# Summing a chunk's weighted neighbour rows and its accumulator on VectorE instead of TensorE, in the two four-head graph attention layers

## The chip, the cores and the metric

One core of a Trainium2 chip runs the whole program. The metric is the device time in microseconds (us) of one execution, the median of several.

## What is computed

A graph has 3,125 nodes with 256 features and 53,125 edges (`src`, `dst`). The reference runs four blocks, each added to `x`: an eight-head graph attention, a mixture-of-experts network with eight experts, two four-head graph attention layers, and a small gated network. Only the two four-head layers are changed:

```python
h = (h_in @ W).reshape(n, 4, 64)
alpha_s = jnp.sum(h * a_s, axis=-1)
alpha_d = jnp.sum(h * a_d, axis=-1)
e = jax.nn.leaky_relu(alpha_s[src] + alpha_d[dst], 0.2)
m = segment_max(e, dst, num_segments=n)
ex = jnp.exp(e - m[dst])
alpha = ex / segment_sum(ex, dst, num_segments=n)[dst]
out = segment_sum(h[src] * alpha[:, :, None], dst, num_segments=n)
return out.reshape(n, 4 * 64) + b
```

So for each node and head: a softmax over the node's neighbours, and the sum of their 64 features weighted by it.

## The kernel before

Nodes are sorted by degree into 25 tiles of 128, one node to a partition. A tile's neighbours are taken in **rounds**: a round is one neighbour of each of the 128 nodes, fetched by one indirect DMA (128 rows of 268 numbers: four heads of 64 features and a one, then the two attention terms). Up to four rounds of one tile make a **chunk** (`ROUNDS` = 4, `TAIL_ROUNDS` = 3), and four chunks, one for each of the four buffer slots (`SLOTS`), make a **block**. A layer has 30 blocks: 21 with chunks of four rounds, then 9 with chunks of three, 120 chunks and 444 gathers. The function `attend` does this for all three attention layers. With `qk` true it is the eight-head layer, with `qk` false one of the four-head layers, which bear the names `gt0` and `gt1` (the profile writes `gt` for both).

The softmax is computed as the chunks come: `peak` holds each node's running maximum and `acc` its running weighted sum, 4 heads by 65 (the last of the 65 is the sum of the weights themselves). What happens to a chunk, by engine:

- GpSimd (POOL) issues its three or four gathers into `rows[:, k]` (line 934), once `weighted` says that the chunk four before, in the same slot, has been read.
- ScalarE (ACT) waits for a slot's gathers, tells VectorE through `chunk_ready`, and issues the load of the slot's next list of indices (`hand_over`, lines 1116 to 1118, 869). Later it computes the exponentials of the shifted scores (line 1132) into `exps`. At a block's end it loads the next list of tiles (line 876). It hands slot k+1 over before it does the exponentials of slot k.
- VectorE (DVE) works in the order that `block_of` writes out by hand. In the step of chunk k it begins the scores of k (lines 981, 987), weights the rows of chunk k-1 into `wv` (`weight_chunk`, line 1014), finishes k's raw scores (line 997), rescales the accumulator of chunk k-2 by the exponential of the change of its peak (`rescale`, line 1027), takes the new peak of k (line 1003), adds chunk k-2's sum to the accumulator (`accumulate`, line 1033) and shifts k's scores (lines 1008, 1009).
- TensorE (PE) sums a chunk's rounds: for each round a product of the identity with `wv[:, k, r]`, accumulated in PSUM in `part` (`sum_block`, line 1183). In float32 the profile shows two matrix instructions for each product.

The accumulator is thus touched three times in a chunk: rescaled in SBUF, summed apart in PSUM by PE, and added.

In `block_of` the rounds of the chunk weighted at k = 0 are always taken as `ROUNDS`, since that chunk belongs to the block before. After a layer, `part` also serves the projection to the next layer (lines 1198 and 1206), and `norm_group` divides by the sum of the weights.

Of the kernel before, what the change touches and what calls it, by code (L numbers as in the profile page):

```python
# [6 lines left out]
ALU, ACT, AX = mybir.AluOpType, mybir.ActivationFunctionType, mybir.AxisListType  # L7

P = 128
# [13 lines left out]
SLOTS = 4  # L23
# [784 lines left out]
def attend(nc, c, g, name, heads, own, own_rows, table, width, qk, bias_row=None, begin=None, onward=None):  # L808
# [13 lines left out]
    ROUNDS, TAIL_ROUNDS = g.rounds, g.rounds - 1  # L822
    MIN_FULL, MAX_FULL = chunk_limits(ROUNDS)
    first_wv, handing = 1 if qk else 0, not qk
    h, dh = heads, D // heads
    av = dh + 1
# [4 lines left out]
    with Mem(nc, name) as m:  # L831
# [4 lines left out]
        idx = m.sb("idx", [P, SLOTS, ROUNDS], I32)  # L836
        listed = m.sb("listed", [1, LISTS * SLOTS, 2], I32)
        score = m.sb("score", [P, SLOTS, ROUNDS + 1, h])
        wv = m.sb("wv", [P, SLOTS, ROUNDS + (1 if qk else 0), h, av])
        recip = m.sb("recip", [P, 2, NT, h])  # L840
        part = m.ps("part", [P, SLOTS, 512])
        exps = None if qk else m.ps("exps", [P, SLOTS, 64])
# [35 lines left out]
        with nc.Block(no_gpsimd_drain=True) as block:  # L878
# [72 lines left out]
            def _(dve):  # L951
# [19 lines left out]
                full, blocks = blocks_of(dve)  # L971
# [39 lines left out]
                def weight_chunk(k, n, rounds):  # L1011
                    dve.wait_ge(exped, n)
                    if not qk:
                        dve.tensor_tensor(wv[:, k, 0:rounds, :, :], rows[:, k, 0:rounds, 0:HW].rearrange("p r (h f) -> p r h f", f=av),  # L1014
                                          exps_of(k)[:, 1:rounds + 1, :].unsqueeze(3).to_broadcast([P, rounds, h, av]), ALU.mult).then_inc(weighted, 1)
                        return
                    row, w = rows[:, k, 0:dve_rounds, v0:v0 + D], wv[:, k, 1:dve_rounds + 1, :, :]
                    dve.tensor_tensor(w[:, :, :, 0:dh], row.rearrange("p r (h d) -> p r h d", d=dh),
                                      w[:, :, :, dh:dh + 1].to_broadcast([P, dve_rounds, h, dh]), ALU.mult).then_inc(weighted, 1)

                def rescale(k, n, t):


                    a = acc[:, bass.ds(t, 1), :, :].rearrange("p a h f -> p (a h) f")
                    dve.wait_ge(added, n)
                    factor = wv[:, k, 0, :, dh:dh + 1] if qk else exps_of(k)[:, 0, :].unsqueeze(2)
                    dve.tensor_tensor(a, a, factor.to_broadcast([P, h, av]), ALU.mult).then_inc(rescaled, 1)

                def accumulate(k, n, t):
                    a = acc[:, bass.ds(t, 1), :, :].rearrange("p a h f -> p (a h f)")  # L1030
                    dve.wait_ge(rescaled, n)
                    dve.wait_ge(part_sum, n)
                    dve.tensor_tensor(a, a, part[:, k, 0:h * av], ALU.add).then_inc(added, 1)  # L1033

                def block_of(i, first, rounds):


                    n = [k + 1 if first else dve.snap(i * SLOTS + (k + 1)) for k in range(SLOTS)]
                    at = 0 if first else dve.snap(i % LISTS * SLOTS)
                    dve.wait_ge(list_in, 32 if first else i * 16 + 16)  # L1040
                    t = [tile_at(at)]
                    for k in range(SLOTS):
                        one, two = (k - 1) % SLOTS, (k - 2) % SLOTS
                        begin_scores(k, n[k], t[k], rounds)
                        if not (first and k < 1):
                            weight_chunk(one, n[k] - 1, rounds if k else ROUNDS)

                        if k < SLOTS - 1:
                            t.append(tile_at(at + (k + 1)))
                        sum_scores(k, n[k], rounds)  # L1050
                        if not (first and k < 2):
                            t_two = t[k - 2] if k >= 2 else tile_at((i + (LISTS - 1)) % LISTS * SLOTS + (SLOTS + k - 2))
                            rescale(two, n[k], t_two)
                        raise_peak(k, n[k], rounds)
                        if not (first and k < 2):
                            accumulate(two, n[k], t_two)
                        shift_scores(k, n[k], t[k], rounds)

                block_of(0, True, ROUNDS)
                if qk:  # L1060
                    dve.wait_ge(own_rest, 16 * (groups - 1))
                with dve.Fori(1, full) as i:
                    block_of(i, False, ROUNDS)
                with dve.Fori(full, blocks) as i:
                    block_of(i, False, TAIL_ROUNDS)
                last = dve.snap(blocks * SLOTS)
                weight_chunk(SLOTS - 1, last, TAIL_ROUNDS)
                for back in (1, 0):
                    t_back = tile_at((blocks + (LISTS - 1)) % LISTS * SLOTS + (SLOTS - 1 - back))
                    rescale(SLOTS - 1 - back, last + (2 - back), t_back)  # L1070
                    accumulate(SLOTS - 1 - back, last + (2 - back), t_back)
                dve.wait_ge(added, last + 3)

                dve.tensor_scalar(recip[:, 0, :, :], acc[:, :, :, dh], 1.0e-30, None, ALU.max).then_inc(den, 1)
# [97 lines left out]

            @block.tensor
            def _(pe):
                pe.sem_inc(part_sum, 2)

                def sum_block(i, rounds):
                    for k in range(SLOTS):
# [5 lines left out]
                                             start=(r == 0), stop=(r == rounds - 1))  # L1184
                        last.then_inc(part_sum, 1)

                full, blocks = blocks_of(pe)
                with pe.Fori(0, full) as i:
                    sum_block(i, ROUNDS)
                with pe.Fori(full, blocks) as i:  # L1190
                    sum_block(i, TAIL_ROUNDS)

                def turn_tile(t):
                    pe.wait_ge(normed if qk else gelued, t // GROUP + 1)
# [1218 lines left out]
```

## Time and profile before

| | us |
|---|---|
| median of 3 runs | 3762.15 |
| lowest and highest of them | 3753.01, 3766.68 |
| span of the profiled execution | 4117.1 |
| gathers of gt0, first to last | 2455.2 to 3129.4 |
| gathers of gt1, first to last | 3199.6 to 3876.5 |

| engine | busy us in the span | share |
|---|---|---|
| PE | 2568.9 | 62% |
| DVE | 2297.6 | 56% |
| POOL | 1687.9 | 41% |
| ACT | 1376.2 | 33% |

The page gives no other time of the profiled execution than its span, so this is its own time. It is 355 us longer than the median of the runs without a profile. The busy times are of the whole program; the two changed layers take the stretch from about 2,450 to 3,890 us, without the projection between them.

### The profile page before, as it was taken

The numbers are of one execution on the slowest core, as the hardware profiler recorded it, in microseconds if no ns is written. First come the engines' busy times: TensorE is split into PE (matmuls) and PEld (weight loads), VectorE is DVE, ScalarE is ACT, GpSimd is POOL, SyncE is SP. The second block draws the span as 40 slices with busy tenths as digits, with TensorE's granted clock in tenths as the row PEclk, the third lists the DMA queues.
The fourth block names the chain that finished last, engine by engine and source line by source line (L and its number), as shares of the span: only waits on it lengthen the run. The fifth ranks groups of instructions, "written<-read, shape, count | busy, mean of one in ns | idle before, by whom it ended". The sixth has DMA issues, their size and how long they took to land. (4 is left out here: it accounts for less than half of the span.)

```text
span 4117.1 us, 65520 instructions
## 1 busy us (share of the span) xinstructions
PE 2568.9 (62%) x14664; PEld 1816.4 (44%) x14665; DVE 2297.6 (56%) x6774; ACT 1376.2 (33%) x4120; POOL 1687.9 (41%) x1822
## 2 busy tenths in 40 slices
PE   7668884987355455645999734444545345445499
PEld 4455233821233333435999623333334233333288
DVE  5867996798577777753111234444455444445642
ACT  1035941587576774311444310000001000000144
POOL 0102001030577676530222356666654666665411
PEclk9579975999676776756999856666677666667689
DMA  4066002811666666422222124333332333333200
GB/s 150 20 167 171 15 3 66 220 64 43 199 181 176 176 177 172 124 78 61 78 76 77 55 84 91 93 88 94 89 88 66 91 91 90 94 90 83 65 27 18
DMA packets 258271, 399.97 MB, mean 97 GB/s; under 512 B 101152, under 2 KB 182606, under 8 KB 257942
## 3 DMA queue, kind: packets, MB, share of 16 engines
q0 software_dynamic: 96144, 291.26, 25.8%
q1 hardware_dynamic: 125814, 103.95, 9.2%
q10 hardware_dynamic: 36240, 3.89, 0.7%
q8 instruction: 34, 0.56, 0.1%
q14 instruction: 39, 0.32, 0.0%
HBM read 355.41 MB, written 43.54 MB: 97 GB/s over the span
## 5 line engine op out<-in xcount | busy, mean ns | idle before, releaser
L1183 PE MATMUL gt_part<-gt_wv,all_ident 128*128 128x260 f32 x1776 | 649.6, 532 | 746.5 <-DVE gt_wv L1014 677.5
L934 POOL DMA_INDIRECT gt_rows<-h_rows,gt_idx x888 | 839.7, 946 | 524.3 <-DVE gt_wv L1014 266.9
L1183 PEld LDWEIGHTS gt_part<-gt_wv,all_ident 128*128 128x128 f32 x1776 | 452.4, 267 | 943.7 <-DVE gt_wv L1014 761.9
L934 POOL DMA_INDIRECT att_rows<-kv_rows,att_idx x444 | 468.0, 1054 | 350.3 <-issue 175.7
L1183 PE MATMUL att_part<-att_wv,all_ident 128*128 128x264 f32 x888 | 339.6, 546 | 369.1 <-ACT att_wv L1137 187.9
L1183 PEld LDWEIGHTS att_part<-att_wv,all_ident 128*128 128x128 f32 x888 | 225.8, 268 | 482.9 <-issue 337.8
L1014 DVE TENSOR_TENSOR gt_wv<-gt_rows,gt_exps 128x1040 f32<-128x1040 f32 (+1 forms) x240 | 280.4, 1168 | 221.1 <-ACT gt_exps L1132 156.0
L1137 ACT ACTIVATE att_wv<-att_rows,att_wv 128x32 f32<-128x32 f32 x1632 | 367.9, 308 | 71.8 <-issue 51.0
L1132 ACT ACTIVATE gt_exps<-gt_score 128x20 f32<-128x20 f32 (+1 forms) x240 | 45.5, 190 | 767.2 <-issue 444.7
L1132 ACT ACT_TABLE_LOAD x63 | 80.8, 1283 | 551.1 <-issue 550.8
L1489 PE MATMUL ex_up<-ex_xe,ex_w 128*128 128x128 f32 x1760 | 208.4, 278 | 12.7 <-DVE ex_xe L1453 12.7
L1489 PEld LDWEIGHTS ex_up<-ex_xe,ex_w 128*128 128x128 f32 x1760 | 207.5, 194 | 16.5 <-DVE ex_xe L1453 13.1
L1498 PE MATMUL ex_down<-ex_w,ex_hid 128*128 128x256 f32 x880 | 199.1, 380 | 0.0
L985 DVE TENSOR_TENSOR att_prod<-att_rows,at_own 128x1056 f32<-128x1056 f32 (+1 forms) x120 | 142.4, 1186 | 79.5 <-SPq L888 45.3
L731 PE MATMUL ixcs_window<-ixcs_oh_c,ixcs_oh_p 128*128 128x512 f16 x416 | 164.3, 418 | 23.8 <-ACT ixcs_oh_p L716 9.6
L716 ACT ACTIVATE ixcs_oh_p<-ixcs_oh_l,edges_value_of_d 128x128 f16<-128x128 f16 x416 | 165.8, 401 | 26.3 <-DVE ixcs_oh_c L669 11.4
L731 PE MATMUL ixcd_window<-ixcd_oh_c,ixcd_oh_p 128*128 128x512 f16 x416 | 160.7, 395 | 18.7 <-ACT ixcd_oh_p L716 3.0
L1498 PEld LDWEIGHTS ex_down<-ex_w,ex_hid 128*128 128x128 f32 x880 | 163.3, 191 | 19.5
L716 ACT ACTIVATE ixcd_oh_p<-ixcd_oh_l,edges_value_of_s 128x128 f16<-128x128 f16 x416 | 165.5, 402 | 17.9 <-DVE ixcd_oh_c L669 6.3
L1033 DVE TENSOR_TENSOR gt_acc<-gt_acc,gt_part 128x260 f32 x240 | 102.0, 425 | 121.5 <-issue 54.4
L1511 ACT ACT_TABLE_LOAD x55 | 70.6, 1283 | 275.5 <-PE ex_up L1489 275.5
L1453 DVE TENSOR_SCALAR ex_xe<-ex_turn,ex_ln_g,ex_ln_b 128x128 f32<-128x128 f32 x112 | 40.8, 406 | 200.0 <-PE ex_turn L1474 179.8
(511 smaller groups left out, 5203.5 us busy)
## 6 DMA issues: line engine op xcount, KB each, us to landing
ex_w<-in_W SPq DMA_DIRECT2D x16, 1024.0 KB, 7.4
ixbs_parts_bc<-key_parts_s SPq DMA_DIRECT2D x14, 1024.0 KB
ixbs_parts_bc<-key_parts_s SPq DMA_DIRECT2D x28, 512.0 KB, 6.2
ixbd_parts_bc<-key_parts_d SPq DMA_DIRECT2D x14, 1024.0 KB
ixbd_parts_bc<-key_parts_d SPq DMA_DIRECT2D x28, 512.0 KB
gt_rows<-h_rows,gt_idx POOLq DMA_INDIRECT x888
att_rows<-kv_rows,att_idx POOLq DMA_INDIRECT x444
y_rows<-ex_y POOLq DMA_DIRECT2D x55, 128.0 KB, 2.0
```

The lines of the kernel that those rows point to most:

```text
L716: act.activation(oh_p[k % RING][:, :], oh_l[k % RING][:, :], ACT.Copy, scale=values[:, bass.ds(i * BATCH + k, 1)]).then_inc(valued, 1)
L731: pe.matmul(window[:, :], oh_p[k % RING][:, :], oh_c[k % RING][:, :], start=False, stop=True, skip_group_check=True).then_inc(summed, 1)
L934: pool.indirect_dma_start(out=rows[:, k, r, :], out_offset=None, in_=table, in_offset=bass.IndirectOffsetOnAxis(ap=idx[:, k, r:r + 1], axi ...
L985: dve.tensor_tensor(of_row, row[:, :, 0:D + h], q, ALU.mult).then_inc(multiplied, 1)
L1014: dve.tensor_tensor(wv[:, k, 0:rounds, :, :], rows[:, k, 0:rounds, 0:HW].rearrange("p r (h f) -> p r h f", f=av), exps_of(k)[:, 1:rounds + ...
L1033: dve.tensor_tensor(a, a, part[:, k, 0:h * av], ALU.add).then_inc(added, 1)
L1132: act.activation(wv[:, k, 0:rounds + 1, :, dh] if qk else exps_of(k)[:, 0:rounds + 1, :], score[:, k, 0:rounds + 1, :], ACT.Exp).then_inc( ...
L1137: last = act.activation(wv[:, k, r + 1, e, 0:dh], rows[:, k, r, v0 + e * dh:v0 + (e + 1) * dh], ACT.Copy, scale=wv[:, k, r + 1, e, dh:dh + 1])
L1183: last = pe.matmul(part[:, k, 0:h * av], c.ident[:, :], wv[:, k, first_wv + r, :, :].rearrange("p h f -> p (h f)"), start=(r == 0), stop=( ...
L1489: last = pe.matmul(up[:, q // 2, (q % 2) * P:(q % 2 + 1) * P], w1[:, k, h, q * P:(q + 1) * P], xe[:, h, :], start=(h == 0), stop=(h == KC ...
L1498: last = pe.matmul(out, hid[:, q, :], w2[:, k, q, :], start=(q == 0), stop=(q == HC - 1))
L1511: act.activation(hid[:, q, :], up[:, q // 2, (q % 2) * P:(q % 2 + 1) * P], ACT.Gelu, bias=b1[:, bass.ds(e, 1), q]).then_inc(act_done, 1)
```

## The change

For the four-head layers (`not qk`):

- `wv` gets one more plane for each slot, behind the rounds.
- `rescale` writes the rescaled accumulator into that plane, and no longer in place.
- `accumulate` is one `tensor_reduce` over the rounds and that plane, written to the accumulator. Its innermost axis is the round, so that it reads one number of each plane in turn, 260 numbers (1,040 bytes) apart.
- PE's loops over the blocks are gone, and with them the semaphore `part_sum`.
- The functions are told how many rounds the chunk has (`before` is the number for a chunk of the block before). For that, the first block of three-round chunks is written out ahead of the loop over the others. The chunk weighted at k = 0 in those others now has three rounds.

The eight-head layer keeps its instructions.

```diff
-        wv = m.sb("wv", [P, SLOTS, ROUNDS + (1 if qk else 0), h, av])
+        wv = m.sb("wv", [P, SLOTS, ROUNDS + 1, h, av])
...
-                def rescale(k, n, t):
+                def rescale(k, n, t, rounds):
                     a = acc[:, bass.ds(t, 1), :, :].rearrange("p a h f -> p (a h) f")
                     dve.wait_ge(added, n)
-                    factor = wv[:, k, 0, :, dh:dh + 1] if qk else exps_of(k)[:, 0, :].unsqueeze(2)
-                    dve.tensor_tensor(a, a, factor.to_broadcast([P, h, av]), ALU.mult).then_inc(rescaled, 1)
+                    if not qk:
+                        dve.tensor_tensor(wv[:, k, rounds, :, :], a, exps_of(k)[:, 0, :].unsqueeze(2).to_broadcast([P, h, av]), ALU.mult).then_inc(rescaled, 1)
+                        return
...
-                def accumulate(k, n, t):
+                def accumulate(k, n, t, rounds):
                     a = acc[:, bass.ds(t, 1), :, :].rearrange("p a h f -> p (a h f)")
+                    if not qk:
+                        dve.wait_ge(state_set, 3)
                     dve.wait_ge(rescaled, n)
+                    if not qk:
+                        dve.tensor_reduce(a, wv[:, k, 0:rounds + 1, :, :].rearrange("p r h f -> p (h f) r"), AX.X, ALU.add).then_inc(added, 1)
+                        return
                     dve.wait_ge(part_sum, n)
                     dve.tensor_tensor(a, a, part[:, k, 0:h * av], ALU.add).then_inc(added, 1)
...
-                            weight_chunk(one, n[k] - 1, rounds if k else ROUNDS)
+                            weight_chunk(one, n[k] - 1, rounds if k else before)
...
-                with dve.Fori(full, blocks) as i:
-                    block_of(i, False, TAIL_ROUNDS)
+                if qk:
+                    with dve.Fori(full, blocks) as i:
+                        block_of(i, False, TAIL_ROUNDS, ROUNDS)
+                else:
+                    block_of(full, False, TAIL_ROUNDS, ROUNDS)
+                    with dve.Fori(dve.snap(full + 1), blocks) as i:
+                        block_of(i, False, TAIL_ROUNDS, TAIL_ROUNDS)
...
-                pe.sem_inc(part_sum, 2)
+                if qk:
+                    pe.sem_inc(part_sum, 2)
...
-                full, blocks = blocks_of(pe)
-                with pe.Fori(0, full) as i:
-                    sum_block(i, ROUNDS)
-                with pe.Fori(full, blocks) as i:
-                    sum_block(i, TAIL_ROUNDS)
+                if qk:
+                    full, blocks = blocks_of(pe)
+                    with pe.Fori(0, full) as i:
+                        sum_block(i, ROUNDS)
+                    with pe.Fori(full, blocks) as i:
+                        sum_block(i, TAIL_ROUNDS)
```

The lines of the changed kernel lie a few below those of before: the rescaling is line 1025, the reduction line 1035.

How VectorE's step stands in the loop over blocks of four-round chunks of layer `gt0` (`gat_own` is the layer's own table, ISA rows are waits and register work), before:

```order
L981 COPY gt_score<-gt_peak 128x4
L987 ISA
L987 TENSOR_TENSOR gt_prod<-gt_rows,gat_own 128x16
L1014 TENSOR_TENSOR gt_wv<-gt_rows,gt_exps 128x1040
L997 SCALAR_TENSOR_TENSOR gt_score<-gt_prod 128x16
L1027 ISA
L1027 TENSOR_TENSOR gt_acc<-gt_acc,gt_exps 128x260
L1003 TENSOR_REDUCE gt_new_peak<-gt_score 128x4
L1033 TENSOR_TENSOR gt_acc<-gt_acc,gt_part 128x260
L1008 TENSOR_TENSOR gt_score<-gt_score,gt_new_peak 128x20
L1009 COPY gt_peak<-gt_new_peak 128x4
```

And now:

```order
L981 COPY gt_score<-gt_peak 128x4
L987 ISA
L987 TENSOR_TENSOR gt_prod<-gt_rows,gat_own 128x16
L1014 TENSOR_TENSOR gt_wv<-gt_rows,gt_exps 128x1040
L997 SCALAR_TENSOR_TENSOR gt_score<-gt_prod 128x16
L1025 ISA
L1025 TENSOR_TENSOR gt_wv<-gt_acc,gt_exps 128x260
L1003 TENSOR_REDUCE gt_new_peak<-gt_score 128x4
L1035 TENSOR_REDUCE gt_acc<-gt_wv 128x260
L1008 TENSOR_TENSOR gt_score<-gt_score,gt_new_peak 128x20
L1009 COPY gt_peak<-gt_new_peak 128x4
```

No instruction has moved and there are as many as before: the rescaling has another target, and the addition from PSUM has become the reduction, ahead of the shift (line 1008) that ScalarE's exponentials wait for.

PE's loop over the blocks of four-round chunks of layer `gt0`, before:

```order
L1188 UNCONDITIONAL_BRANCH
L1188 ISA
L1183 MATMUL gt_part<-gt_wv,all_ident 128x260 x4
L1179 REGISTER_ALU
L1183 MATMUL gt_part<-gt_wv,all_ident 128x260 x4
L1179 REGISTER_ALU
L1183 MATMUL gt_part<-gt_wv,all_ident 128x260 x4
L1179 REGISTER_ALU
L1183 MATMUL gt_part<-gt_wv,all_ident 128x260 x4
L1188 ISA
L1188 COMPARE_AND_BRANCH
```

And now, PE's rows from the end of the work ahead of the layer (line 1545) on:

```order
L1545 UNCONDITIONAL_BRANCH
L1183 UNCONDITIONAL_BRANCH
L1210 MATMUL gt_part<-all_ident,gat_own 128x128 x4
L1218 MATMUL gt_part<-all_ga,gt_a_t 128x264 x2
L1210 MATMUL gt_part<-all_ident,gat_own 128x128 x2
```

Both loops are gone from PE, and its first work in the layer is the projection (lines 1210 and 1218 now, 1198 and 1206 before).

## Rows read from the trace of the kernel before

**Rows 1.** The page's costliest groups: instructions, busy us and mean ns, idle before.
```profile
L1183 PE MATMUL gt_part<-gt_wv,all_ident 128*128 128x260 f32 x1776 | 649.6, 532 | 746.5 <-DVE gt_wv L1014 677.5
L1014 DVE TENSOR_TENSOR gt_wv<-gt_rows,gt_exps 128x1040 f32<-128x1040 f32 (+1 forms) x240 | 280.4, 1168 | 221.1 <-ACT gt_exps L1132 156.0
L1033 DVE TENSOR_TENSOR gt_acc<-gt_acc,gt_part 128x260 f32 x240 | 102.0, 425 | 121.5 <-issue 54.4
```
**Rows 2.** Engines by stretch, gt0: the four-round blocks, then the three-round blocks.
```profile
core 0: us, PE busy (x) PEld busy (x) DVE busy (x) ACT busy (x) POOL busy (x), PEclk, DMA share, GB/s
2455.00:2959.00 504.00, 231.03 (x644) 165.00 (x645) 222.32 (x731) 42.38 (x102) 318.25 (x337) 0.66 0.36 92
2959.00:3145.00 186.00, 91.93 (x246) 60.87 (x244) 99.17 (x353) 8.60 (x40) 101.59 (x108) 0.70 0.33 81
```
**Rows 3.** Timeline of POOL: two four-round blocks' starts (start us, length).
```profile
2600.29 0.94 POOL L934 DMA_INDIRECT gt_rows<-h_rows,gt_idx  x1 [3.62 <-DVE gt_wv L1014]
...
2619.04 0.95 POOL L934 DMA_INDIRECT gt_rows<-h_rows,gt_idx  x1 [0.30 <-issue]
2623.58 0.94 POOL L934 DMA_INDIRECT gt_rows<-h_rows,gt_idx  x1 [3.60 <-DVE gt_wv L1014]
```
**Rows 4.** Timeline of POOL in three-round blocks of gt0.
```profile
3076.55 0.94 POOL L934 DMA_INDIRECT gt_rows<-h_rows,gt_idx  x1 [4.78 <-DVE gt_wv L1014]
...
3090.30 0.95 POOL L934 DMA_INDIRECT gt_rows<-h_rows,gt_idx  x1 [0.30 <-issue]
3096.06 0.95 POOL L934 DMA_INDIRECT gt_rows<-h_rows,gt_idx  x1 [4.82 <-DVE gt_wv L1014]
```
**Rows 5.** Timeline of DVE in the block of rows 3.
```profile
2601.76 1.23 DVE L1014 TENSOR_TENSOR gt_wv<-gt_rows,gt_exps 128x1040 f32<-128x1040 f32 x1
...
2604.44 1.23 DVE L1014 TENSOR_TENSOR gt_wv<-gt_rows,gt_exps 128x1040 f32<-128x1040 f32 x1
...
2609.84 1.23 DVE L1014 TENSOR_TENSOR gt_wv<-gt_rows,gt_exps 128x1040 f32<-128x1040 f32 x1
...
2621.56 1.24 DVE L1014 TENSOR_TENSOR gt_wv<-gt_rows,gt_exps 128x1040 f32<-128x1040 f32 x1 [5.12 <-DMA at_own<-q_ordered]
```
**Rows 6.** Timeline of DVE in the block of rows 4.
```profile
3077.92 0.95 DVE L1014 TENSOR_TENSOR gt_wv<-gt_rows,gt_exps 128x780 f32<-128x780 f32 x1
...
3080.42 0.95 DVE L1014 TENSOR_TENSOR gt_wv<-gt_rows,gt_exps 128x780 f32<-128x780 f32 x1
...
3085.06 1.23 DVE L1014 TENSOR_TENSOR gt_wv<-gt_rows,gt_exps 128x1040 f32<-128x1040 f32 x1
```
**Rows 7.** Timeline of ACT in the block of rows 3.
```profile
2606.99 1.24 ACTq L876 DMA_DIRECT2D gt_listed<-tile_of_d  x1
2610.71 0.36 ACTq L869 DMA_DIRECT2D gt_idx<-neighbours_d  x1
2620.04 1.28 ACT L1132 ACT_TABLE_LOAD   x1 [13.17 <-issue]
...
2621.33 0.19 ACT L1132 ACTIVATE gt_exps<-gt_score 128x20 f32<-128x20 f32 x1
```
**Rows 8.** Groups of DVE by line and shape: its reductions.
```profile
L1003 DVE TENSOR_REDUCE gt_new_peak<-gt_score 128x4 f32<-128x20 f32 x168 | 30.5, 182 | 6.5 <-issue 6.0
L1003 DVE TENSOR_REDUCE gt_new_peak<-gt_score 128x4 f32<-128x16 f32 x72 | 12.4, 172 | 4.3 <-issue 3.9
L312 DVE TENSOR_REDUCE ixad_rank<-ixad_sel 128x25 f32<-128x3200 f32 x1 | 3.5, 3489 | 0.0
L294 DVE TENSOR_REDUCE ixas_deg<-ixas_counts 128x25 f32<-128x800 f32 x1 | 1.6, 1646 | 0.0
L322 DVE TENSOR_REDUCE ixas_sdeg<-ixas_by_tile 128x25 f32<-128x625 f32 x1 | 1.3, 1305 | 0.0
L306 DVE TENSOR_REDUCE ixas_within<-ixas_equal 128x25 f32<-128x625 f32 x1 | 0.8, 807 | 0.0
```
**Rows 9.** Waits of DVE in gt0: us in total, times, longest us.
```profile
DVE gt_acc L1033 <- PE gt_part L1183: 9.8, 8, 3.3
```

More of the change, by code:

```diff
@@ L1019, in weight_chunk, with block_of @@
                                       w[:, :, :, dh:dh + 1].to_broadcast([P, dve_rounds, h, dh]), ALU.mult).then_inc(weighted, 1)
-                def rescale(k, n, t):
+                def rescale(k, n, t, rounds):
                     a = acc[:, bass.ds(t, 1), :, :].rearrange("p a h f -> p (a h) f")
                     dve.wait_ge(added, n)
-                    factor = wv[:, k, 0, :, dh:dh + 1] if qk else exps_of(k)[:, 0, :].unsqueeze(2)
-                    dve.tensor_tensor(a, a, factor.to_broadcast([P, h, av]), ALU.mult).then_inc(rescaled, 1)
-                def accumulate(k, n, t):
+                    if not qk:
+                        dve.tensor_tensor(wv[:, k, rounds, :, :], a, exps_of(k)[:, 0, :].unsqueeze(2).to_broadcast([P, h, av]), ALU.mult).then_inc(rescaled, 1)
+                        return
+                    dve.tensor_tensor(a, a, wv[:, k, 0, :, dh:dh + 1].to_broadcast([P, h, av]), ALU.mult).then_inc(rescaled, 1)
+                def accumulate(k, n, t, rounds):
                     a = acc[:, bass.ds(t, 1), :, :].rearrange("p a h f -> p (a h f)")
+                    if not qk:
+                        dve.wait_ge(state_set, 3)
                     dve.wait_ge(rescaled, n)
+                    if not qk:
+                        dve.tensor_reduce(a, wv[:, k, 0:rounds + 1, :, :].rearrange("p r h f -> p (h f) r"), AX.X, ALU.add).then_inc(added, 1)
+                        return
                     dve.wait_ge(part_sum, n)
                     dve.tensor_tensor(a, a, part[:, k, 0:h * av], ALU.add).then_inc(added, 1)
-                def block_of(i, first, rounds):
+                def block_of(i, first, rounds, before=None):
                     n = [k + 1 if first else dve.snap(i * SLOTS + (k + 1)) for k in range(SLOTS)]
@@ L1052, in block_of @@
                             t_two = t[k - 2] if k >= 2 else tile_at((i + (LISTS - 1)) % LISTS * SLOTS + (SLOTS + k - 2))
-                            rescale(two, n[k], t_two)
+                            rescale(two, n[k], t_two, rounds if k >= 2 else before)
                         raise_peak(k, n[k], rounds)
                         if not (first and k < 2):
-                            accumulate(two, n[k], t_two)
+                            accumulate(two, n[k], t_two, rounds if k >= 2 else before)
                         shift_scores(k, n[k], t[k], rounds)
@@ L1062, in _ @@
                 with dve.Fori(1, full) as i:
-                    block_of(i, False, ROUNDS)
-                with dve.Fori(full, blocks) as i:
-                    block_of(i, False, TAIL_ROUNDS)
+                    block_of(i, False, ROUNDS, ROUNDS)
+                if qk:
[5 more added lines that the diff above has]
+                        block_of(i, False, TAIL_ROUNDS, TAIL_ROUNDS)
                 last = dve.snap(blocks * SLOTS)
@@ L1069, in _ @@
                     t_back = tile_at((blocks + (LISTS - 1)) % LISTS * SLOTS + (SLOTS - 1 - back))
-                    rescale(SLOTS - 1 - back, last + (2 - back), t_back)
-                    accumulate(SLOTS - 1 - back, last + (2 - back), t_back)
+                    rescale(SLOTS - 1 - back, last + (2 - back), t_back, TAIL_ROUNDS)
+                    accumulate(SLOTS - 1 - back, last + (2 - back), t_back, TAIL_ROUNDS)
                 dve.wait_ge(added, last + 3)
```

## The prediction

> **What bounds the kernel now.** I first read the page's costliest groups. PE's identity products are the largest of all, 649.6 us busy, while VectorE's addition from PSUM takes 425 ns each [rows 1]. That invites the thought that removing PE's 650 us is a gain. The view by stretches says otherwise: in the four-round blocks of gt0 POOL is busy 318 of 504 us, PE 231, DVE 222, and PE's granted clock is 0.66, a mix of its two levels, 1.2 and 2.4 GHz [rows 2]. PE works in the shadow of something: of gt0's 120 additions only 8 waited for PE, 9.8 us together [rows 9].
>
> The timeline of POOL shows the frame. From the first gather of a block to its sixteenth are 18.75 us, so 1.25 us for each, without a gap; then POOL stands still 3.6 us until a chunk is weighted [rows 3]. In the three-round blocks it is the same with twelve gathers and 4.8 us [rows 4]. Without the stops a block would take 16 x 1.25 = 20.0 us, or 12 x 1.25 = 15.0 us, and a layer 21 x 20 + 9 x 15 = 555 us; from the first gather to the last the trace has 674 and 677 us.
>
> What ends the stop is VectorE's weighting (line 1014), and what VectorE waited for is ScalarE's exponential. ScalarE loads indices at 2610.71 and computes the next exponential only at 2621.33, after 13.17 us that the profile puts down to no one [rows 7]. Its exponentials stand behind the hand-over of the next slot, whose gathers are the block's fifth to eighth, issued by POOL from 2605.3 to 2609.0 (2600.29 + 4 x 1.25 and + 7 x 1.25) and no reason to wait until 2621. So I read these as stretches in which the issuing itself was slow. They lie in the profiled execution: two layers at 555 us instead of 674 and 677 would be 241 us shorter, and the execution is 355 us longer than the median of the others (the first attention layer gathers in the same way and can hold the rest). I take it that the measured runs are near the floor of 20.0 and 15.0 us a block, set by POOL, and count the change against that floor. The Trainium skill ("NOTIFIC — the notification-queue block", 7.1) says that the block which writes trace records can hold an engine back when its own pipeline is full. The length of the profiled execution agrees; no row here shows that it is the cause.
>
> **VectorE's own pace before.** When data is there, from one weighting to the next are 2.68 us with four rounds, and 5.40 us across the end of a block [rows 5], where VectorE waits for ScalarE's list load (1.24 us) and its first hand-over [rows 7]. A four-round block thus needs 3 x 2.68 + 5.40 = 13.4 us of VectorE's chain against POOL's 20.0. With three rounds: 2.50 and 4.64 us [rows 6], 12.1 us against 15.0.
>
> **What the change costs, part by part.**
> - PE's products go: 1776 instructions. What hid them was POOL's pace, so this gives nothing but the few waits of rows 9, which are behind POOL's pace too. The wait for PE in the drain of a layer goes (one product group, about 1 us for each layer) and is repaid by the last two reductions. PE's first work after the layer now comes from a standstill, but it stood still for 6 us before too; I count nothing.
> - The rescaling has the same 260 elements and another target: nothing. If writing SBUF elsewhere cost 50 ns, VectorE's block would grow by 0.2 us.
> - The three-round loop weights three rounds instead of four at k = 0: 1.23 to 0.95 us [rows 6], -0.28 us in 8 of 9 blocks. The block written out separately adds no instruction that is executed.
> - The addition (425 ns) becomes a reduction of 5 x 260 = 1300 elements, or 4 x 260 = 1040. This is the price that decides, and no row has it. Four rows bracket it [rows 8]. Where the elements lie side by side, 625 take 807 ns and 3200 take 3489 ns: 1.04 ns for each and 156 ns once. The reduction of line 322 has the same 625 elements in groups of 25, but reads across the rows, 100 bytes apart: 1305 ns; line 294 also reads 100 bytes apart and takes 1646 ns for 800: 1.95 ns for each and 86 ns once. The new one reads 1,040 bytes apart, so it is nearest to these two: 1300 x 1.95 + 86 = **2.62 us**, and 2.11 us with 1040. Lower end: side by side, 1.51 and 1.24 us. Upper end: the small strided reductions of line 1003 grow by 10 ns for 4 elements, 2.5 ns for each, which gives 3.4 and 2.7 us.
>
> What a page makes of the price: by the Trainium skill ("VectorE: DVE Perf Modes", Mode 1x (REGULAR) — the baseline, and the tier table) a float32 reduction runs at one element a cycle and "weird strides" cost nothing, which as an estimate is the lower end, about 1.5 us. Lines 306 and 322 speak against it: same size, same grouping, 1305 against 807 ns. "SBUF — State Buffer" (Door 1) says that an access which crosses to a new 16-byte line pays; by it 2.6 us would stand, and the trace agrees.
>
> **The sum.** The reduction lies between VectorE's rescaling and its shift of the scores, so it lengthens every step: 2.62 - 0.43 = +2.20 us, or 2.11 - 0.43 = +1.69 us.
> - Four-round block: 13.4 + 4 x 2.20 = 22.2 us on VectorE, against POOL's 20.0. VectorE becomes the bound, by 2.2 us; 21 blocks: 46 us.
> - Three-round block: 12.1 + 4 x 1.69 - 0.28 = 18.6 us against 15.0, by 3.6 us; 9 blocks: 32 us.
> - Per layer 78 us, two layers 157 us. A layer's first block has no crossing (5.40 - 2.68 = 2.7 us for each layer), and some of the old stops may be real and absorb a little: **+150 us**.
>
> Against the profiled execution's 4117 us this is the same amount if its slow stretches stay hidden as they are; against the median, 3762 + 150 = **3912 us**, +4.0%. VectorE turns from 13.4 of 20.0 us into the bound when the reduction takes over 2.07 us with four rounds ((20.0 - 13.4) / 4 + 0.43), and over 1.21 us with three.
>
> **The rivals.**
> 1. *The reduction is as quick as one over neighbours.* Then 1.51 us: a four-round block needs 13.4 + 4 x 1.08 = 17.8 us, under 20.0, and a three-round block 12.1 + 4 x 0.81 - 0.28 = 15.1 us, about POOL's pace. 2 x 9 x 0.1 us and the drains: at most +7 us, 3769 us, no change that can be told. For it: every price is over its groups, and the new one's stride is not among them. Against it: all the strided reductions of rows 8. Chance 0.10.
> 2. *Faster: the slow stretches are in the measured runs too, and PE's loops feed them.* PE, ScalarE and VectorE run short loops at once; if PE's instructions are what makes ScalarE issue slowly, they end with its loops. Then a layer goes from 674 us to VectorE's 21 x 22.2 + 9 x 18.6 = 634 us: -40 us for each, 3682 us. It decides if the measured runs hold over 79 us of stops in a layer and these end. Against: the 355 us have to be somewhere, and PE issues far more elsewhere. Chance 0.05.
> 3. *Slower by more: the stretches are real, stay, and add.* ScalarE's slow stretch hides one of four steps; the other three grow openly: 3 x 2.20 x 21 + 3 x 1.69 x 9 = 184 us for each layer, 4130 us. For it: in rows 5 to 7 the stop begins only when the steps are done. Chance 0.07.
> 4. *The forecast's mechanism, with smaller crossings.* If ScalarE's hand-over at a block's end is quicker without the profiler, 1.5 us instead of 2.7 us, blocks take 21.0 and 17.4 us: +2 x (21 + 22) = +86 us, 3848 us. With the reduction's upper end, +2.95 and +2.28 us, they take 25.2 and 20.9 us: +2 x (109 + 53) = +324 us, 4086 us. Both belong to the forecast; its own range is 3830 to 3990 us.
>
> **How the numbers follow.** VectorE becomes the bound: 0.78. Rival 1: 0.10, rival 2: 0.05, rival 3: 0.07. The likeliest gives 3912 us. The range from 3765 to 4010 us takes in the forecast's own and rival 1, and leaves out rivals 2 and 3 and the reduction's upper end, together 0.15 to 0.2. A measurement of this kernel can tell about 0.5% from no change, 19 us. Faster by more than that is rival 2 alone, 0.05; within it is rival 1, 0.10; slower is the rest, 0.85.
>
> **What would show it.** Right: the reduction's group (240 of them) at a mean of about 2.5 us, VectorE's busy time in the program up by 240 of these less 102 us, some 490 us; from one weighting to the next about 4.9 us when data is there; POOL in a four-round block with gaps in front of single chunks, not one stop of 3.6 us; VectorE without idle time but at a block's end. Each of PE's 1776 products gone, and its clock low through the layers. Wrong: a reduction near 1.5 us (rival 1); a stage shorter than 674 us and a median under 3743 us (rival 2); a reduction of 2.6 us with VectorE still idle for 5 us in each block, and a median over 4050 us (rival 3).

## The result and the profile after

| | us |
|---|---|
| median after, 4 runs | 3941.53 (3936.98 to 3945.78) |
| median before, 4 runs beside them | 3759.11 (3753.01 to 3766.68) |
| ratio | 1.0483, 95% interval 1.0464 to 1.0502 |
| predicted | 3912, range 3765 to 4010 |
| span of the profiled execution after | 3938.8 |

The kernel is slower by 182 us. The forecast was +150 us.

The page of the changed kernel, its head and the groups that answer to [rows 1] (busy us, mean ns | idle before):

```profile
span 3938.8 us, 61586 instructions
...
PE 1905.8 (48%) x12888; PEld 1359.9 (35%) x12889; DVE 2733.4 (69%) x6774; ACT 1369.5 (35%) x4120; POOL 1682.0 (43%) x1822
...
L934 POOL DMA_INDIRECT gt_rows<-h_rows,gt_idx x888 | 839.2, 945 | 456.1 <-issue 271.0
...
L1035 DVE TENSOR_REDUCE gt_acc<-gt_wv 128x1300 f32 (+1 forms) x240 | 550.5, 2294 | 5.6 <-issue 0.8
...
L1014 DVE TENSOR_TENSOR gt_wv<-gt_rows,gt_exps 128x1040 f32<-128x1040 f32 (+1 forms) x240 | 275.7, 1149 | 7.8 <-ACT gt_exps L1142 7.6
```

PE has lost 663 us of work and the kernel is longer. VectorE has gained 436 us: 550.5 us of reductions in place of 102.0 us of additions, less 5 us of weighting and a few us elsewhere. The idle time in front of VectorE's weighting is 7.8 us where it was 221 us [rows 1]: VectorE hardly waits for an exponential any more, and ScalarE now waits for VectorE's shifted scores.

The reduction by shape, for the price that [rows 8] bracketed:

```profile
L1035 DVE TENSOR_REDUCE gt_acc<-gt_wv 128x1300 f32 x168 | 412.6, 2456 | 4.1 <-issue 0.8
L1035 DVE TENSOR_REDUCE gt_acc<-gt_wv 128x1040 f32 x72 | 137.9, 1915 | 1.5
```

The engines in the four-round and the three-round blocks of gt0, as in [rows 2] (busy, and the granted clock):

```profile
core 0: us, PE busy (x) PEld busy (x) DVE busy (x) ACT busy (x) POOL busy (x), PEclk, DMA share, GB/s
2339.00:2800.00 461.00, 0.00 (x0) 0.00 (x0) 380.39 (x729) 42.38 (x102) 316.71 (x336) 0.50 0.40 100
2800.00:2990.00 190.00, 0.00 (x0) 0.00 (x0) 149.93 (x341) 7.12 (x38) 102.90 (x109) 0.50 0.32 80
```

VectorE is busy 83% and 79% of the stretch, PE not at all, and its clock is at the lower level, 1.2 GHz, throughout. From the first gather of gt0 to the last are 641.8 us, in gt1 640.8 us.

VectorE's timeline over one four-round block (start us, length), answering to [rows 5]:

```profile
2504.45 1.23 DVE L1014 TENSOR_TENSOR gt_wv<-gt_rows,gt_exps 128x1040 f32<-128x1040 f32 x1
...
2506.17 0.43 DVE L1025 TENSOR_TENSOR gt_wv<-gt_acc,gt_exps 128x260 f32<-128x260 f32 x1 [0.40 <-issue]
...
2506.82 2.45 DVE L1035 TENSOR_REDUCE gt_acc<-gt_wv 128x1300 f32 x1
2509.20 0.16 DVE L1008 TENSOR_TENSOR gt_score<-gt_score,gt_new_peak 128x20 f32<-128x20 f32 x1
...
2509.84 1.23 DVE L1014 TENSOR_TENSOR gt_wv<-gt_rows,gt_exps 128x1040 f32<-128x1040 f32 x1
...
2511.41 0.43 DVE L1025 TENSOR_TENSOR gt_wv<-gt_acc,gt_exps 128x260 f32<-128x260 f32 x1 [0.26 <-issue]
...
2514.96 1.23 DVE L1014 TENSOR_TENSOR gt_wv<-gt_rows,gt_exps 128x1040 f32<-128x1040 f32 x1
...
2519.74 1.23 DVE L1014 TENSOR_TENSOR gt_wv<-gt_rows,gt_exps 128x1040 f32<-128x1040 f32 x1
...
2526.60 0.18 DVE L987 TENSOR_TENSOR gt_prod<-gt_rows,gat_own 128x16 f32<-128x16 f32 x1 [2.12 <-ACTq L1127]
2526.69 1.23 DVE L1014 TENSOR_TENSOR gt_wv<-gt_rows,gt_exps 128x1040 f32<-128x1040 f32 x1
```

The steps are 5.39, 5.12, 4.78 and 6.95 us, 22.24 us for the block. The reduction sits between the rescaling (line 1025) and the shift (line 1008), so it is open in each. The idle 2.12 us is the block's end: ScalarE has first to load the new list before it hands over (line 1127). That wait starts only when VectorE has done its last shift, so it isn't hidden.

POOL, answering to [rows 3]: its gathers in the same stretch.

```profile
2506.47 0.94 POOL L934 DMA_INDIRECT gt_rows<-h_rows,gt_idx  x1 [0.72 <-DVE gt_wv L1014]
...
2511.86 0.94 POOL L934 DMA_INDIRECT gt_rows<-h_rows,gt_idx  x1 [0.70 <-issue]
...
2528.71 0.94 POOL L934 DMA_INDIRECT gt_rows<-h_rows,gt_idx  x1 [2.04 <-DVE gt_wv L1014]
```

In place of one stop of 3.6 us a block, as [rows 3] have it, there are gaps of 0.7 us ahead of single chunks and one of 2 us. The bound has gone over from POOL to VectorE.

### The profile page after: what moved, and what is told of

It reads as the page before. It is cut to its first block and busy times, and to the rows that moved or that the text cites. A ratio compares the mean times of both kernels' runs of the same rounds, so it can differ in the third digit from the quotient of the medians.

```text
span 3938.8 us, 61586 instructions
## 1 busy us (share of the span) xinstructions
PE 1905.8 (48%) x12888; PEld 1359.9 (35%) x12889; DVE 2733.4 (69%) x6774; ACT 1369.5 (35%) x4120; POOL 1682.0 (43%) x1822
## 5 line engine op out<-in xcount | busy, mean ns | idle before, releaser
L934 POOL DMA_INDIRECT att_rows<-kv_rows,att_idx x444 | 452.2, 1018 | 286.6 <-DMA att_idx<-neighbours_s 134.1
L1035 DVE TENSOR_REDUCE gt_acc<-gt_wv 128x1300 f32 (+1 forms) x240 | 550.5, 2294 | 5.6 <-issue 0.8
L1147 ACT ACTIVATE att_wv<-att_rows,att_wv 128x32 f32<-128x32 f32 x1632 | 358.9, 307 | 3.9
L1755 PE MATMUL f_turn<-all_ident,f_rows 128*128 128x128 f32 x50 | 9.6, 313 | 694.2 <-DVE f_rows L788 692.7
L1210 PE MATMUL gt_part<-all_ident,gat_own 128*128 128x128 f32 x50 | 10.4, 297 | 674.8 <-ACT gat_own L1174 674.8
```

Source lines behind the costliest of these rows:

```text
L934: pool.indirect_dma_start(out=rows[:, k, r, :], out_offset=None, in_=table, in_offset=bass.IndirectOffsetOnAxis(ap=idx[:, k, r:r + 1], axi ...
L1035: dve.tensor_reduce(a, wv[:, k, 0:rounds + 1, :, :].rearrange("p r h f -> p (h f) r"), AX.X, ALU.add).then_inc(added, 1)
L1147: last = act.activation(wv[:, k, r + 1, e, 0:dh], rows[:, k, r, v0 + e * dh:v0 + (e + 1) * dh], ACT.Copy, scale=wv[:, k, r + 1, e, dh:dh + 1])
```

## The experiments

Medians are of four to six executions (`before_again` is one alone) beside runs of the kernel before on the same chip; those gave 3756.4 (first four kernels below), 3756.1 (`three_adds`, `dose_one`, `dose_two`, `reduce_four_only`) and 3755.2 us (the other four). A block's period is the median from its first gather to the next block's.

**The kernel before, profiled again.** No edit. The forecast had taken the measured runs to be at POOL's pace and the slow stretches of [rows 3, 7] to belong to that one execution.

> The kernel before, profiled once more. Theory (the slow stretches of the first profile belong to that execution and its recording, not to the kernel): the span can come out anywhere between the measured 3759 us and 4117 us; if it comes out near 3759, POOL's gathers go through a four-round block in 20.0 us and a three-round block in 15.0 us, 555 to 570 us from a layer's first gather to its last. Rival (PE's loops make ScalarE issue slowly, in every run of this kernel): 4100 us or so again, 674 us from first gather to last.

One time, 3766.39 us. The page's span, and the engines in two stretches that together hold gt0 (columns as above):

```profile
span 3764.8 us, 65520 instructions
```

```profile
2357.00:2694.00 337.00, 189.32 (x516) 129.67 (x516) 182.80 (x588) 34.20 (x82) 254.47 (x270) 0.74 0.45 110
2694.00:2915.00 221.00, 137.51 (x362) 92.16 (x360) 134.12 (x482) 15.13 (x57) 165.12 (x175) 0.73 0.44 110
```

POOL is busy three quarters of both. Blocks take 20.0 and 15.0 us, and from the first gather to the last are 553.5 us in both layers, against 674 and 677 in the first profile and 555 worked out. So the stops were that execution's, not the kernel's. The two layers hold 244 of the 352 us by which the two spans differ; another 98 us lie ahead of the first gather of gt0. POOL waited for the weighting 6 times in gt0, 1.8 us together; in the changed kernel it is 47 times, 86.5 us:

```profile
POOL gt_rows L934 <- DVE gt_wv L1014: 1.8, 6, 0.3
```

```profile
POOL gt_rows L934 <- DVE gt_wv L1014: 86.5, 47, 4.3
```

The first fence is the kernel before, the second the change (us, times, longest). The layer grew by 88 us, and that wait by 85. What made the first execution slow no run shows.

**The change with PE's products put back**, their sums waited for and not used.

```diff
-                if qk:
-                    full, blocks = blocks_of(pe)
-                    with pe.Fori(0, full) as i:
-                        sum_block(i, ROUNDS)
...
+                full, blocks = blocks_of(pe)
+                with pe.Fori(0, full) as i:
+                    sum_block(i, ROUNDS)
...
                     if not qk:
+                        dve.wait_ge(part_sum, n)
                         dve.tensor_reduce(a, wv[...], AX.X, ALU.add).then_inc(added, 1)
```

> The changed kernel with PE's identity products put back; the accumulator is still formed by the reduction, and the products' results are read by nobody, but the reduction waits for them as the addition did. Theory (PE's work was covered and its removal gives nothing): 3941 us, within 15 us. Rival (PE's loops slow the issuing of the others): 40 us a layer longer, about 4020 us.

3943.44 us (3941.09 to 3945.91), ratio to before 1.0498 [1.0464, 1.0533], blocks 22.3 and 19.7 us: the time of the change, with 708 us of PE's products in it. Taking them away gave nothing, and it costs nothing elsewhere.

**The rounds laid innermost**, so that the reduction reads neighbours.

```diff
-        wv = m.sb("wv", [P, SLOTS, ROUNDS + 1, h, av])
+        wv = m.sb("wv", [P, SLOTS, ROUNDS + 1, h, av] if qk else [P, SLOTS, h, av, ROUNDS + 1])
...
+   weighting writes wv[:, k, :, :, 0:rounds].rearrange("p h f r -> p r h f")
+   rescaling writes wv[:, k, :, :, rounds]
+   reduction reads  wv[:, k, :, :, 0:rounds + 1].rearrange("p h f r -> p (h f) r")
```

> The changed kernel with wv laid out so that a number's rounds lie side by side. Theory (the stride of the read sets the price): the reduction falls from 2.46 to about 1.5 us with four rounds and from 1.92 to about 1.2 us with three, VectorE's blocks fall under or to POOL's 20.0 and 15.0 us, and the time to 3759 to 3790 us, if writing the weighted rows with a stride of five numbers costs nothing. Rival (the price comes from the 260 small groups): the reduction stays at 2.4 us and the time at 3941 us.

3888.34 us (3884.88 to 3892.13), ratio 1.035 [1.0316, 1.0384]; blocks 21.2 and 19.2 us. Far above what was expected. VectorE's groups by shape:

```profile
L1014 DVE TENSOR_TENSOR gt_wv<-gt_rows,gt_exps 128x1040 f32<-128x1040 f32 x168 | 335.5, 1997 | 6.9 <-ACT gt_exps L1142 6.8
L1035 DVE TENSOR_REDUCE gt_acc<-gt_wv 128x1300 f32 x168 | 253.2, 1507 | 20.0 <-DVE gt_wv L1025 5.2
L1025 DVE TENSOR_TENSOR gt_wv<-gt_acc,gt_exps 128x260 f32<-128x260 f32 x240 | 146.6, 611 | 3.5 <-issue 2.8
...
L1035 DVE TENSOR_REDUCE gt_acc<-gt_wv 128x1040 f32 x72 | 89.0, 1236 | 7.2
```

The reduction is at 1507 and 1236 ns, where the line through the side-by-side rows of [rows 8] puts 1.51 and 1.24 us. So the spacing makes up 0.95 us of the 2.46. But the weighting now writes each number 20 bytes from the last and takes 1997 ns instead of 1230, the rescaling 611 instead of 422. What the read saved in a four-round chunk, the writes took back: 0.95 us against 0.96. Still the kernel is 53 us faster than the change. The first two steps of a block are shorter, 4.82 and 4.69 us with four rounds instead of 5.39 and 5.12, the other two are not. The row of the rescaling shows a part of it: the idle time ahead of it is 3.5 us, where the change has 47.3:

```profile
L1025 DVE TENSOR_TENSOR gt_wv<-gt_acc,gt_exps 128x260 f32<-128x260 f32 x240 | 101.3, 422 | 47.3 <-issue 46.9
```

That fits a longer weighting which covers VectorE's own issuing behind it. The idle time ahead of the reduction grew in turn, from 5.6 to 27.2 us, so this makes 22 of the 53 us; where the rest comes from isn't shown.

**The reduction behind the shift of the scores**, and so out of ScalarE's way.

```diff
                         raise_peak(k, n[k], rounds)
-                        if not (first and k < 2):
+                        if qk and not (first and k < 2):
                             accumulate(two, n[k], t_two, rounds if k >= 2 else before)
                         shift_scores(k, n[k], t[k], rounds)
+                        if not qk and not (first and k < 2):
+                            accumulate(two, n[k], t_two, rounds if k >= 2 else before)
```

> The changed kernel with the reduction behind the shift of the scores instead of ahead of it. Theory (at a block's end VectorE idles for ScalarE's exponential, list load and hand-over, and the reduction could lie there): four-round blocks go from 22.2 to POOL's 20.0 us, three-round blocks from 19.7 to about 17.8 us: 2 x (21 x 2.2 + 9 x 1.9) = 127 us less, 3815 us. Rival (only VectorE's busy time counts): 3941 us, no change.

3802.85 us (3798.45 to 3808.81), ratio 1.013 [1.0097, 1.0164]: of the 182 us, 139 are gone, with the same instructions at the same lengths. Blocks are 20.0 and 16.85 us. The end of a block and the first step of the next:

```profile
2511.69 2.45 DVE L1035 TENSOR_REDUCE gt_acc<-gt_wv 128x1300 f32 x1
...
2512.05 1.23 ACTq L876 DMA_DIRECT2D gt_listed<-tile_of_d  x1
...
2514.32 0.18 DVE L987 TENSOR_TENSOR gt_prod<-gt_rows,gat_own 128x16 f32<-128x16 f32 x1
2514.42 1.23 DVE L1014 TENSOR_TENSOR gt_wv<-gt_rows,gt_exps 128x1040 f32<-128x1040 f32 x1
...
2520.38 1.24 DVE L1014 TENSOR_TENSOR gt_wv<-gt_rows,gt_exps 128x1040 f32<-128x1040 f32 x1 [0.90 <-ACT gt_exps L1144]
```

ScalarE loads its list (line 876) while VectorE does the reduction, and VectorE goes on to the next score with hardly any idle time, where the change has 2.12 us. What is left is 0.90 us ahead of the weighting in the next block's first step. A four-round block is back at POOL's 20.0 us; in three-round blocks VectorE stays above 15.0.

**The reduction in four-round chunks alone, and in three-round chunks alone**, with PE's products in; the other chunks are rescaled in place and added from PSUM as before.

```diff
-                    if not qk:
+                    if not qk and rounds == ROUNDS:
                         dve.tensor_tensor(wv[:, k, rounds, :, :], a, ..., ALU.mult).then_inc(rescaled, 1)
...
-                    if not qk:
+                    if not qk and rounds == ROUNDS:
                         dve.tensor_reduce(a, wv[...], AX.X, ALU.add).then_inc(added, 1)
```

(`ROUNDS` stands for the first, `TAIL_ROUNDS` for the second.)

> The changed kernel with PE's products in place, and the reduction in chunks of four rounds alone; chunks of three are rescaled in place and take PE's sum. Theory: four-round blocks at 22.2 us, three-round blocks at 15.0: 3756 + 2 x 21 x 2.2 = 3850 us. Rival (a block's lateness is made up in the three-round blocks behind it): under 3800 us.

> The counterpart of reduce_four_only: PE's products in place, the reduction in chunks of three rounds alone. Theory: four-round blocks at 20.0 us, three-round blocks at 19.7: 3756 + 2 x 9 x 4.7 = 3841 us, and with reduce_four_only's 108 us the two parts make the whole, 185 us. Rival (the parts overlap): less than 60 us.

3863.81 us (3856.87 to 3871.55), ratio 1.0277 [1.026, 1.0294], with blocks of 22.2 and 15.0 us; and 3838.70 us (3829.55 to 3843.44), ratio 1.0217 [1.02, 1.0235], with blocks of 20.0 and 19.7 us. The parts cost 108 and 83 us; together 191, against 187 for both at once. By blocks they are 2 x 21 x 2.24 = 94 us and 2 x 9 x 4.7 = 85 us. The 14 us missing in the first lie where the two kinds meet: the first two three-round blocks of gt0 take 22.57 and 16.93 us from gather to gather, since VectorE is still at chunks of four rounds, 9.5 us more than twice 15.0. A layer's first block, at 20.1 us, gives 2.2 us back.

**A dose of VectorE time in the kernel before**, ahead of the addition, where the change has its reduction: no change of layout, of PE or of the sum. The first pair adds a private SBUF table to itself, 900 numbers (about 1.08 us, under the threshold of four rounds and over that of three), or 1880 and 1370 (about the reduction less the addition).

```diff
                 def accumulate(k, n, t, rounds):
+                    if not qk:
+                        size = 900
+                        dve.wait_ge(dosed, n)
+                        dve.tensor_tensor(dose[:, 0, 0:size], dose[:, 1, 0:size], dose[:, 1, 0:size], ALU.add).then_inc(dosed, 1)
```

> The kernel before, PE's products and all, with one more VectorE instruction of 900 numbers ahead of the addition, about 1.0 us of its chain in every step; its result is read by nobody. Theory (only what lifts VectorE's block over POOL's is seen): a four-round block needs 13.4 + 4.0 = 17.4 us and stays hidden; a three-round block 12.1 + 4.0 = 16.1 to 17 us against 15.0: 2 x 9 x 1.1 to 2 = 20 to 36 us more, 3776 to 3792 us. Rival (each us on VectorE counts): 240 us more, 3996 us.

> The kernel before with the extra instruction sized like what the reduction adds: 1880 numbers with four rounds (about 2.0 us), 1370 with three (about 1.5 us). Theory (the change costs what VectorE's occupancy costs, whatever the instruction): as the changed kernel, 3941 us, within 20; the three-round loop's four-round weighting adds 2 x 9 x 0.28 = 5 us. Rival (the stride, the missing PE or the SBUF target of the rescaling cost in another way as well): well under 3941 us, 3850 or so.

Both missed, to the slow side: 3871.83 us (3867.41 to 3878.69), ratio 1.0308 [1.0289, 1.0327], and 4019.29 us (4016.81 to 4024.09), ratio 1.0697 [1.0679, 1.0715]. The doses themselves had the length meant, 1087 ns, and 2110 and 1578. It is POOL's gathers that grew, from 945 ns in the mean to 1059 and 1222:

```profile
L935 POOL DMA_INDIRECT gt_rows<-h_rows,gt_idx x888 | 940.0, 1059 | 289.4 <-issue 249.7 <-DVE gt_wv L1019 27.4 <-DMA gt_idx<-neighbours_d 12.3
```

The timeline of the same kernel around one dose: a gather issued while it runs takes 1.37 us instead of 0.95.

```profile
2509.42 1.09 DVE L1039 TENSOR_TENSOR gt_dose<-gt_dose 128x900 f32<-128x900 f32 x1
2509.96 1.37 POOL L935 DMA_INDIRECT gt_rows<-h_rows,gt_idx  x1 [0.30 <-issue]
```

A gather and the 0.30 us behind it then take 1.36 and 1.52 us in the mean, and sixteen of them 21.8 and 24.4 us; the four-round blocks of these kernels take 21.8 and 24.0. So this dose was not clean: both operands lie in SBUF, unlike those of the kernel's weighting and addition. The second pair takes the second operand from PSUM (the exponentials, broadcast) and multiplies, with about the same lengths.

```diff
-   dve.tensor_tensor(dose[:, 0, 0:size], dose[:, 1, 0:size], dose[:, 1, 0:size], ALU.add)
+   dve.tensor_tensor(dose[:, 0, 0:size], dose[:, 1, 0:size], exps_of(k)[:, 0, :].unsqueeze(2).to_broadcast(...), ALU.mult)
```

> dose_one again, its extra instruction of 900 numbers now with one operand in SBUF and the other in PSUM. Theory (dose_one was slow because an instruction that reads two operands of SBUF holds POOL's gathers up, 1.06 us instead of 0.95 on the mean): the gathers are back at 0.95 us, four-round blocks at 20.0 us, three-round blocks at 16 to 17.4 us: 3776 to 3800 us. Rival (ScalarE's table load at a block's start makes VectorE's chain longer than 13.4 us, and that is what dose_one showed): 3870 us again.

> dose_two with one operand in PSUM. Theory (the change costs what VectorE's occupancy costs, whatever the instruction): four-round blocks at 22.2 us, three-round blocks at 19.7 us, 3941 us, within 20. Rival (the reduction or the missing PE cost in another way too, or the dose costs in another): over 3980 or under 3900 us.

3796.06 us (3789.98 to 3801.58), ratio 1.0108 [1.0091, 1.0125]; and 3923.08 us (3911.31 to 3927.28), ratio 1.0445 [1.0423, 1.0467].

```profile
L935 POOL DMA_INDIRECT gt_rows<-h_rows,gt_idx x888 | 839.8, 946 | 318.4 <-issue 265.2 <-DVE gt_wv L1019 41.9 <-DMA gt_idx<-neighbours_d 11.4
```

With the small one, gathers are back at 946 ns and four-round blocks at 20.0 us: 1.08 us are absorbed there, and cost 2.2 us in a three-round block (17.2). With the large one (2101 and 1568 ns) blocks take 21.9 and 19.3 us, nearly the change's own 22.2 and 19.7. VectorE's time in that place is thus enough to explain 168 of the 182 us, with no reduction, no new plane and no missing PE in the kernel.

**Three short additions in place of the reduction**, each over neighbouring numbers: planes 0 and 1 plus planes 2 and 3; with four rounds plane 4 (the rescaled accumulator) plus plane 0; and the last one into the accumulator, behind the shift.

```diff
+   dve.tensor_tensor(wv[:, k, 0:2, :, :], wv[:, k, 0:2, :, :], wv[:, k, 2:4, :, :], ALU.add)
+   dve.tensor_tensor(wv[:, k, 4, :, :], wv[:, k, 4, :, :], wv[:, k, 0, :, :], ALU.add)
-   dve.tensor_reduce(a, wv[...], AX.X, ALU.add)
+   dve.tensor_tensor(a, flat[:, 4 if rounds == ROUNDS else 0, :], flat[:, 1, :], ALU.add)
```

> The changed kernel with the reduction written as additions of neighbouring planes of wv, between the other instructions of the step: with four rounds one of 520 and two of 260 numbers, with three rounds one of 520 and one of 260; no PE. Theory (VectorE may sum the rounds at no cost as long as its block stays under POOL's): one of 260 takes about 0.34 us of the chain and one of 520 about 0.6, so a step grows by about 0.9 us with four rounds and 0.6 with three, a block to about 17 and 14.5 us, under 20.0 and 15.0: 3756 us, within 15. Rival (any sum on VectorE is dearer than PE's, since each addition waits for the one before): 20 to 60 us more than the kernel before.

3790.73 us (3781.68 to 3794.22), ratio 1.0086 [1.0065, 1.0106], blocks 20.4 and 15.3 us. The sum costs 0.70 + 0.43 + 0.43 = 1.56 us instead of 2.46, but these too have two operands in SBUF, and the gathers average 968 ns. That lifts POOL's own floor to 16 and 12 times 1.27 us, 20.3 and 15.2, about what the blocks take. The time is some 20 us above the upper end of what was expected and inside the rival's range, but not for the rival's reason: ahead of the last addition VectorE is idle for 3.3 us in the whole program.

**Four-round chunks alone, and behind the shift**: the order of `late_reduce` on `reduce_four_only`.

> The reduction behind the shift of the scores and in chunks of four rounds alone, PE's sum in chunks of three. Theory (a block under POOL's 20.0 us costs nothing): four-round blocks at 20.0 us as in late_reduce, three-round blocks at 15.0 us: 3756 us, within 12. Rival (POOL pays for the longer steps in another way): 20 us or more above the kernel before.

3759.67 us (3756.01 to 3768.87), ratio 1.0016 [1.0, 1.0032], blocks 20.0 and 15.0 us. A reduction of 2.46 us in each four-round chunk costs nothing when nothing waits behind it. It gains nothing either: POOL's 16 x 1.25 us hold. None of these kernels is faster than the one before.

## Why the prediction was right

Right were the direction, the mechanism and, within the range, the size; several terms of the sum were off.

- **The floor.** "The measured runs are near the floor of 20.0 and 15.0 us" was the boldest step. The second profile shows 20.0 and 15.0. Rival 2, faster because stops end, fell with it, and rival 3 (the stretches are real and add, 4130 us) too.
- **PE's products: nothing.** Shown by putting them back, 3943.4 against 3941.5 us. PE's work outside them is 1905.8 us, and in the second profile of the kernel before 2567.8 - 657.6 = 1910.2: it didn't suffer from the standstill.
- **The reduction's price**, 2.62 and 2.11 us, measured 2.46 and 1.92: too high by 0.16 and 0.20 us. Taking the rows with a spacing of 100 bytes as the nearest was right, and the side-by-side end (rival 1, 3769 us) holds only for another layout: `rounds_innermost` meets that end to 5 ns. The "lower end", one element a cycle by the tier table of the Trainium skill ("VectorE: DVE Perf Modes"), is thus a price for neighbours, not for this spacing. That an access to a new line of 16 bytes pays, as the Trainium skill ("SBUF — State Buffer", Door 1) says, agrees with the 0.95 us; no run has a spacing under 16 bytes, so the size of the line is not shown.
- **Four-round blocks**, 22.2 us predicted, 22.24 measured, by errors that cancel, which is luck. The crossing comes out at 6.95 instead of 7.60 us. The three other steps take 15.3 instead of 14.6 us, though each reduction is 0.16 us cheaper: VectorE stands idle in the first two, 0.40 and 0.26 us ahead of the rescaling, which is 0.66 of the 1.2 us by which they exceed 3 x (2.68 + 2.03).
- **Three-round blocks**, 18.6 us predicted, 19.7 measured: this is the step that failed, in two terms. The working took 2.50 us, the shortest step, for all that don't cross. And it took off 0.28 us for the shorter weighting at k = 0, which its 12.1 us do not contain, since the 4.64 us of [rows 6] end where that weighting begins. Timeline of VectorE in the changed kernel's three-round block:

```profile
2897.49 0.96 DVE L1014 TENSOR_TENSOR gt_wv<-gt_rows,gt_exps 128x780 f32<-128x780 f32 x1
...
2899.20 0.43 DVE L1025 TENSOR_TENSOR gt_wv<-gt_acc,gt_exps 128x260 f32<-128x260 f32 x1 [0.68 <-issue]
...
2902.20 0.96 DVE L1014 TENSOR_TENSOR gt_wv<-gt_rows,gt_exps 128x780 f32<-128x780 f32 x1
...
2903.76 0.42 DVE L1025 TENSOR_TENSOR gt_wv<-gt_acc,gt_exps 128x260 f32<-128x260 f32 x1 [0.52 <-issue]
...
2906.76 0.96 DVE L1014 TENSOR_TENSOR gt_wv<-gt_rows,gt_exps 128x780 f32<-128x780 f32 x1
...
2910.72 0.96 DVE L1014 TENSOR_TENSOR gt_wv<-gt_rows,gt_exps 128x780 f32<-128x780 f32 x1
```

The third step is 3.96 us, which is 2.50 + 1.92 - 0.43 to within 0.03. The first two are 4.71 and 4.56: VectorE stands still 0.68 and 0.52 us ahead of the rescaling, for nothing that the profile shows but its own issuing. The kernel before has such idle time in the same steps, 0.41 and 0.56 us in its first profile, in rows that the working left out. In the second profile:

```profile
2862.54 0.42 DVE L1027 TENSOR_TENSOR gt_acc<-gt_acc,gt_exps 128x260 f32 x1 [0.42 <-issue]
...
2865.55 0.42 DVE L1027 TENSOR_TENSOR gt_acc<-gt_acc,gt_exps 128x260 f32 x1 [0.52 <-issue]
```

It cost nothing there, under POOL's pace, and became open when VectorE was the bound. The shorter weighting at k = 0 saved nothing at all: 0.42 us of idle time behind a weighting of 1.23 us have become 0.68 behind one of 0.96. From the predicted 18.6 us, 0.28 not taken off, 1.20 of idle time, 0.8 less for four cheaper reductions and 0.3 more in the crossing (6.4 us against 4.64 + 1.49) give 19.6. With the measured blocks the sum is 21 x 2.24 + 9 x 4.7 = 89 us a layer, 179 us, against 182 measured.

- **The crossing** (2.7 us in which ScalarE loads its list and hands over) was added in full, since nothing covers it while the reduction is ahead of the shift. Measured it is 2.2 us with four rounds (6.95 - 4.78) and about 2.4 with three. `late_reduce` shows it from the other side: covered, the block is back at POOL's 20.0 us.
- **The threshold**, over 1.65 us of added time with four rounds and 0.8 with three: a dose of 1.08 us left four-round blocks at 20.0 and lengthened three-round ones by 2.2 us, on the right side of both. In the three-round block the working gives 12.1 + 4 x 1.08 - 15.0 = 1.4 us: short by 0.8 us, about the idle time that it left out (0.41 and 0.52 us ahead of the rescaling in that kernel).
- Of the signs named, one failed: VectorE is idle inside a block too, and not at its end alone. The others held: a mean of 2294 ns against about 2.5 us, VectorE's busy time +436 against some +490 us, POOL's single gaps, steps of 4.8 to 5.4 against 4.9 us, and PE's clock low.

## What to carry to other kernels

The largest busy time can belong to work that costs nothing; before moving it, work out each engine's own pace for one block and compare. Moving a sum onto the engine that comes second is paid four times a block, and the place of the moved instruction counts as much as its length: in front of what another engine waits for it was open, behind it the greater part was hidden. Sum the second engine's chain over all steps of a block with their idle time, not over the shortest one; and when a profiled execution is much longer than the median, profile again before explaining its waits.

## What the runs showed that was not expected

- **VectorE with both operands in SBUF slows POOL's indirect gathers.** A gather takes 945 ns in the mean; with one such instruction of 1.09 us in a chunk 1059, with one of 2.1 us 1222 (the longest 2.9 us), with the shorter additions of `three_adds` 968, and 946 with the second operand in PSUM. Sorted by whether they overlap such an instruction in time, the gathers of `dose_one` take 1228 ns (355 of them) and 945 (the other 533), and those of `dose_two` 1533 and 946; 332 gathers that overlap the dose with an operand in PSUM take 946. The eight-head layer's product (line 985) reads two tables in SBUF; its gathers take 1162 ns in the mean where they overlap it and 988 where they don't, all together 1064, in the second profile of the kernel before:

```profile
L934 POOL DMA_INDIRECT att_rows<-kv_rows,att_idx x444 | 472.2, 1064 | 286.5 <-DMA att_idx<-neighbours_s 133.1 <-issue 132.1 <-ACT att_wv L1137 20.3
```

  The Trainium skill ("SBUF — State Buffer", Who interferes with whom) says that such an instruction contends with a GpSimd instruction that reads SBUF, and infers that writing descriptors is not held up by it. Here an indirect gather, which reads its indices from SBUF, is held up; which part of it waits these runs do not tell. The reduction of this change has one input, and the 575 gathers that overlap it take 945 ns.
- **A spacing costs VectorE on the write side too**: 1040 numbers written 20 bytes apart take 1997 ns, side by side 1230; 260 take 611 and 422. The rule of the Trainium skill that the prediction weighed ("SBUF — State Buffer", Door 1) would have it so, each number lying in another line of 16 bytes; the runs agree, with this one spacing.
- **One profiled execution of the kernel before was 355 us longer than its median**, and the next, of the same kernel, was at it.
